# Moving y's second half by one token: shift products on TensorE replaced by transfers from SBUF to SBUF

## The chip, the cores and the metric

The kernel runs on one core of a Trainium2 chip. The metric is the device time of one execution in microseconds (us), taken as the median of several runs; lower is better.

## The reference

Three blocks are added to x (4 batches x 512 tokens x 256 channels, float32), each behind a layer normalization: causal self-attention with 16 heads, a linear cross-attention with 16 heads, and two layers of a local-attention transformer. Only the two layers matter here. Each of them does, for its input x:

```
def shift_token(t):
    t1, t2 = jnp.split(t, 2, axis=-1)
    t2 = jnp.pad(t2, ((0, 0), (1, 0), (0, 0)))[:, :-1]
    return jnp.concatenate([t1, t2], axis=-1)

h = shift_token(x);  q, k, v = split(h @ wqkv);  ...        # 8 heads, windows of 128 tokens
x = x + local_attention(q, k, v) @ wo
h = shift_token(x)                                          # the move that is changed
h = (h - h.mean(-1)) / sqrt(h.var(-1) + 1e-05) * lg + lb
a, g = split(h @ w1 + b1);  x = x + (a * gelu(g)) @ w2 + b2
```

shift_token moves the second 128 channels of every token down by one token: token n gets those of token n - 1, and token 0 gets zeros.

## The kernel before, in words

The two layers run as eight steps m = 0 to 7, one per layer and batch. y, the running x of the layers, lies in SBUF as 128 partitions x 4 batches x 4 token tiles x 256 channels: token 128 t + p is partition p of tile t. A step projects q, k, v, does four pairs of heads (scores in two parts Sa and Sb, exponentials, transposes T in two halves, values AV), sums the pairs into the output product wo in two halves of two token tiles, and adds each half to y (`add_to_y`, L1382 on VectorE). The MLP of the step follows interleaved with the next step's attention: statistics, shift, normalization into hn, transposes of hn (hnT), the first product w1 with its gates, the second product w2.

The move by one token is a matter of partitions, which VectorE and ScalarE do not cross, so before the change TensorE does it. `shifted_half` (L1827, L1829) multiplies y's second halves by a matrix that has ones one place off the diagonal, and a second product carries partition 127 of tile t to partition 0 of tile t + 1. The result is a bank of PSUM called "sh". `mlp_stats` takes the statistics of the first half from y (L1390), `mlp_norm` those of the second half from the bank (L1396) and joins them (L1399); GpSimd makes rstd (`mlp_rstd`, L806 and L808); `mlp_apply` writes hn, the second half from the bank (L1408) and the first from y (L1412).

Every engine works through one list written out by hand, in order: a START, UNIT and ENTRY list for the first two blocks, then STEP_PE, STEP_DVE, STEP_ACT and STEP_POOL, repeated for each step with a lead (@1 is the next step's item, @-1 the last one's), and CLOSE lists for the end. An item whose input is not there stops all that stand behind it on its engine. Banks of PSUM go round in groups: "g" (2, 5, 6, 7) serves q, k, v, wo, w1, w2, AV and sh in the order of TensorE's list, "t" (3, 4) the transposes. In PSUM banks 0 and 1 Sb of a pair follows Sa, and TensorE may write Sb only when VectorE has read Sa.

SyncE issues all transfers, on one queue, in the order of its program: it loads layer 1's weights as the last products of layer 0 are done, reads x2 back, and stores y. It too stops at each wait. hn shares its place in SBUF with hnT and with the gates gl of the MLP; VectorE has read the last of them before it adds the next step's output sums.

Of the kernel before, what the change touches and what calls it, by code (L numbers as in the profile page):

```python
# [10 lines left out]
ALU = mybir.AluOpType  # L11
# [3 lines left out]
P = 128  # L15
# [51 lines left out]
def constants():  # L67

    ident = np.eye(P, dtype=np.float32)
    i = np.arange(P)[:, None]  # L70
    j = np.arange(P)[None, :]
    causal = np.zeros((P, S), np.float32)
    causal[:, S - P:] = np.where(j <= i, 0.0, NEG)
    local = np.concatenate([np.where(i <= j, 0.0, NEG), np.where(j <= i, 0.0, NEG)], 1).astype(np.float32)
    heads = (i // XDH == j // XDH).astype(np.float32)
    half = np.arange(0, FDH, 2, dtype=np.float32)
    inv_freq = (1.0 / np.float32(10000.0) ** (half / np.float32(FDH))).astype(np.float32)
    t = np.arange(S, dtype=np.float32)
    freqs = t[:, None] * inv_freq[None, :]
    freqs = np.concatenate([freqs, freqs], -1)  # L80
    base = ((half + np.float32(0.4 * FDH)) / np.float32(1.4 * FDH)).astype(np.float32)
    power = ((t - S // 2) / np.float32(W // 2)).astype(np.float32)
    scale = (base[None, :] ** power[:, None]).astype(np.float32)
    scale = np.concatenate([scale, scale], -1)
    cos, sin = np.cos(freqs), np.sin(freqs)
    sign = np.where(np.arange(FDH) < FDH // 2, -1.0, 1.0).astype(np.float32)
    rot = np.stack([cos * scale, sin * sign * scale, cos / scale, sin * sign / scale])
    rot = rot.reshape(4, T, P, FDH).transpose(2, 0, 1, 3).astype(np.float32)
    shift = np.zeros((P, 2, P), np.float32)
    shift[:, 0, :] = i == j - 1  # L90
    shift[P - 1, 1, 0] = 1.0
    return {"c_ident": ident, "c_causal": causal, "c_local": local, "c_heads": heads, "c_shift": shift,
            "c_rot": np.ascontiguousarray(rot)}


def build(nc, a, out, x2_dram, w_dram, tab_dram):

    with ExitStack() as ctx:
        def sem(name):
            return ctx.enter_context(nc.semaphore(name))  # L100
# [102 lines left out]
        b1 = sbt(ctx, "b1", [P, DEPTH, 2, NF])  # L203
        shift = sbt(ctx, "shift", [P, 2, P])
        hnT_hi = sbt(ctx, "hnT_hi", [P, E2, S], F32R)
# [103 lines left out]
        def unit_at(u):  # L309
# [29 lines left out]
        ENTRY_DVE = ("sA.30 r.29.0 z.28 sB.30 r.29.1 pk.31 t.29.0 t.29.2 pq.31 t.29.4 sA.31 r.30.0 z.29 sB.31 "  # L339
# [21 lines left out]
        STEP_PE = ("q2@1 hnT@-1 v2@1 k2@1 Ta1 Sa3 hid0@-1 Tb1 hid1@-1 Tqk1@1 Sb3 hid2@-1 q3@1 hid3@-1 k3@1 "  # L361
                   "Tqk2@1 hid4@-1 hid5@-1 AV1 Ta2 v3@1 hT@2 w20@-1 Tqk3@1 q0@2 Tb2 Sa0@1 AV2 Sb0@1 k0@2 "
                   "Ta3 q1@2 w21@-1 Tb3 k1@2 Sa1@1 AV3 Sb1@1 Ta0@1 wo0 wo1 v0@2 sh Tb0@1 v1@2 Sa2@1 AV0@1 "
                   "Sb2@1 Tqk0@2")
        STEP_DVE = ("Tqk3 Tb2@-1 Sa0 fb3@-1 q0@1 w20@-2 Sb0 k0@1 Ta3@-1 q1@1 w21@-2 Tb3@-1 fa0 Sa1 k1@1 Sb1 "
# [3 lines left out]
        STEP_ACT = ("Tqk0@1 AV0 q2@1 v1@1 hnT@-1 ea2 k2@1 Ta1 v2@1 eb2 Tb1 hid0@-1 hs0@-1 hid1@-1 Tqk1@1 "  # L369
                    "hid2@-1 hs1@-1 hs2@-1 q3@1 hid3@-1 k3@1 Tqk2@1 hs3@-1 hid4@-1 hid5@-1 hs4@-1 hs5@-1 Ta2 "  # L370
# [3 lines left out]
        CLOSE_PE = ("T.29.0 hnT.6 Sa.31 T.29.1 w1.6.0 w1.6.1 Sb.31 AV.29 T.30.0 w1.6.2 T.30.1 w1.6.3 w1.6.4 "  # L374
                    "AV.30 T.31.0 wo_early.7.0 T.31.1 w1.6.5 AV.31 wo_early.7.1 wo.7.0 wo.7.1 sh.7 w2.6.0 "
                    "hnT.7 w2.6.1 w1.7.0 w1.7.1 w1.7.2 w1.7.3 w1.7.4 w1.7.5 w2.7.0 w2.7.1")
        CLOSE_DVE = ("soft.27.1 Tqk.7.3 w2.5.0 T.26.1 Sa.28 T.27.0 Sb.28 T.27.1 soft.28.0 Sa.29 Sb.29 w2.5.1 "
# [6 lines left out]
        CLOSE_ACT = ("AV.28 T.29.0 hnT.6 T.29.1 exp.30.0 w1.6.0 w1.6.1 exp.30.1 AV.29 T.30.0 exp.31.0 w1.6.2 "  # L384
                     "w1.6.3 T.30.1 exp.31.1 AV.30 T.31.0 hs.6.0 w1.6.4 hs.6.1 T.31.1 w1.6.5 hs.6.2 hs.6.3 "
                     "AV.31 hs.6.4 hs.6.5 hnT.7 w1.7.0 hs.7.0 w1.7.1 w1.7.2 w1.7.3 hs.7.1 w1.7.4 hs.7.2 "
                     "hs.7.3 w1.7.5 hs.7.4 hs.7.5")
        CLOSE_POOL = ("sum.0 soft.30.1 soft.31.0 soft.31.1 last.6 norm.7 last.7 sum.1")
        MLP = ("stats", "sh", "norm", "apply", "hnT", "hT")

# [83 lines left out]
        for what, *at in pe_order:  # L474
# [31 lines left out]
            if what == "w1":  # L506
# [3 lines left out]
                else:  # L510
                    plan["w1a", at[0], at[1]] = plan["w1g", at[0], at[1]]
            if what == "sh":
                turn(("sh", *at), "g")
            if what == "Tqk":
# [42 lines left out]
        def _(sp):  # L557
# [115 lines left out]
            for l in range(DEPTH):  # L673
                sp.dma_start(lng[:, l, :], a["ln_g"][l]).then_inc(ld_small, 16)
                sp.dma_start(lnb[:, l, :], a["ln_b"][l]).then_inc(ld_small, 16)
                sp.dma_start(b1[:, l, :, :], a["b1"][l]).then_inc(ld_small, 16)
            sp.dma_start(shift[:, :, :], a["c_shift"]).then_inc(ld_shift, 16)

            wait_full(sp, plan["q", B - 1, T - 1])
            layer_wqkv_lo(1, 0)  # L680
# [9 lines left out]
            layer_wqkv_hi(1, 2)  # L690
            for tp in range(2):
                wait_read(sp, plan["wo", B - 1, tp])
            layer_wo(1)
            wait_full(sp, plan["w1a", B - 1, NF - 1])
            layer_w1(1)
            for tp in range(2):
                wait_full(sp, plan["w2", B - 1, tp])
            layer_w2(1)
            wait_full(sp, plan["v", STEPS - 1, T - 1])
            sp.wait_ge(l_ssm, 2 * T * STEPS)  # L700
            for b in range(B):
# [377 lines left out]
        def _(dve):  # L1079
# [312 lines left out]
            def mlp_norm(m):  # L1392

                bank = wait_full(dve, plan["sh", m])
                for t in range(T):
                    dve.bn_stats(stats[:, 0, t, 6:12], bank[:, t * P:(t + 1) * P]).then_inc(f_stats, 1)  # L1396
                dve.wait_ge(f_stats, 2 * T * (m + 1))
                for t in range(T):
                    dve.bn_aggr(mv[:, 0, t, :], stats[:, 0, t, :]).then_inc(f_mv, 1)  # L1399

            def mlp_apply(m):
                b = m % B
                dve.wait_ge(f_mv, T * (m + 1))
                dve.wait_ge(f_rstd, m + 1)
                use = plan["sh", m]
                bank = psum[use[0]]
                for t in range(T):
                    ins = dve.tensor_scalar(hn[:, t, P:D], bank[:, t * P:(t + 1) * P], mv[:, 0, t, 0:1],  # L1408
                                            rstd[:, 0, t:t + 1], ALU.subtract, ALU.mult)
                ins.then_inc(read[use[0]], 1)  # L1410
                for t in range(T):
# [114 lines left out]
        def _(pe):  # L1526
# [291 lines left out]

            def shifted_half(m):

                if m == 0:
                    pe.wait_ge(ld_shift, 16)
                for tp in range(2):
                    wait_read(pe, plan["wo", m, tp])
                use = plan["sh", m]
                bank = wait_free(pe, use)
                mm(bank[:, :].rearrange("p (t e) -> p t e", e=P), shift[:, 0, :], y[:, m % B, :, P:D], start=True,  # L1827
                   stop=False, skip_group_check=True)
                mm(bank[:, P:T * P].rearrange("p (t e) -> p t e", e=P), shift[:, 1, :], y[:, m % B, 0:T - 1, P:D],  # L1829
                   start=False, stop=True, skip_group_check=True).then_inc(full[use[0]], 1)  # L1830

            def transposed_norm(m):
# [38 lines left out]
            for what, *at in pe_order:  # L1871
# [40 lines left out]
                if what == "wo":  # L1912
                    output_part(*at, range(FPAIRS - 1, FPAIRS) if at[0] == STEPS - 1 else range(FPAIRS))
                if what == "sh":
                    shifted_half(*at)
                if what == "hnT":
# [81 lines left out]
```

## Time and profile before

| | us |
|---|---|
| median of three runs | 1153.77 (1152.77 to 1156.58) |
| the profiled execution's own time | 1154.38 |
| its span, first to last instruction | 1152.6 |
| TensorE busy | 1124.3 (98%) |
| VectorE busy | 790.9 (69%) |
| ScalarE busy | 691.6 (60%) |
| GpSimd busy | 610.0 (53%) |

The span is what the profile's times count in; the execution's own time has 1.8 us more around it. The chain that ended last is 90% TensorE. The first two blocks end at about 600 us; the eight steps take the rest, and their output sums are added to y at 612, 688, 764, 840, 916, 992, 1061 and 1107 us.

### The profile page before, as it was taken

The page shows a single profiled execution, that of the slowest core. Times are in us where ns is not written, and L with a number is a line of the kernel's source. Part 1 is how long each engine was busy: PE and PEld are TensorE (multiplying, and loading weights), DVE is VectorE, ACT ScalarE, POOL GpSimd, SP SyncE. Part 2 cuts the span into 40 slices and gives each one's busy share as a digit, 9 for nine tenths or more (in the row PEclk, how much of TensorE's full clock was granted, in tenths as well). Part 3 has the DMA queues.
Part 4 walks back from the last instruction along what each step waited for, and adds up shares of the span by engine and source line. Part 5 has one row for each costly group of instructions (what it writes and reads, how often), then busy time and mean ns, then how long its engine had stood idle before and what let it go on. Part 6 is the DMA issues. An engine that isn't in the chain of part 4 may idle for free.

```text
span 1152.6 us, 20639 instructions
## 1 busy us (share of the span) xinstructions
PE 1124.3 (98%) x7114; PEld 874.4 (76%) x7114; DVE 790.9 (69%) x2417; ACT 691.6 (60%) x1712; POOL 610.0 (53%) x641
## 2 busy tenths in 40 slices
PE   8999999999999999999999999999999999999997
PEld 6777777777777766767667887877878878787676
DVE  6867677667767356778897677768667686675553
ACT  3668677777767224453676647657656566575832
POOL 1456666666664322049896446557465474573330
PEclk9999999999999999999999999999999999999999
DMA  7003333323210401030040001200002100001010
GB/s 255 1 2 132 100 109 113 123 93 123 89 71 2 164 19 55 1 112 22 19 176 1 2 1 36 94 1 1 1 19 99 55 1 1 1 32 42 19 38 18
DMA packets 30310, 64.72 MB, mean 56 GB/s; under 512 B 3840, under 2 KB 16256, under 8 KB 29696
## 3 DMA queue, kind: packets, MB, share of 16 engines
q1 hardware_dynamic: 30208, 63.41, 15.7%
q8 instruction: 58, 0.95, 0.3%
q14 instruction: 44, 0.36, 0.1%
HBM read 41.04 MB, written 22.36 MB: 55 GB/s over the span
## 4 chain that ended last, share of the span: by engine, by line
PE 90%; DVE 4%; POOL 2%; ACT 2%; issue 1%; DMA 0%; DVEq 0%; ACTq 0%; POOLq 0%
PE psum L1532 48%; PE psum L1633 7%; PE psum L1598 6%; PE psum L1615 6%; PE psum L1765 5%; PE psum L1814 5%; PE psum L1799 4%; PE psum L1781 4%; PE psum L1747 2%; PE psum L1827 1%; PE psum L1838 1%; PE psum L1721 1%; POOL rn L780 1%; PE psum L1829 0%; DVE y L1091 0%
## 5 line engine op out<-in xcount | busy, mean ns | idle before, releaser
L735 POOL TENSOR_TENSOR probs<-probs,rden 128x128 f32<-128x128 f32 (+3 forms) x256 | 177.6, 725 | 80.6 <-DVE rden L1149 80.6
L974 ACT ACTIVATE lp<-lp,lneg,rn 128x256 f32<-128x256 f32 (+1 forms) x256 | 143.6, 568 | 11.6 <-DVE lneg L1366 11.5
L890 ACT ACTIVATE probs<-probs,negmax 128x128 f32<-128x128 f32 (+3 forms) x256 | 139.9, 553 | 5.8 <-DVE negmax L1144 5.8
L1134 DVE CUSTOM_DVE_ANT_0 probs<-psum,causal 128x128 f32<-128x128 f32 (+3 forms) x256 | 110.3, 487 | 19.4 <-PE psum L1598 19.3
L768 POOL TENSOR_TENSOR lp<-lp,lrden 128x128 f32<-128x128 f32 x64 | 25.6, 400 | 165.8 <-DVE lrden L1371 165.8
L780 POOL TENSOR_TENSOR rn<-ssm,neg_half 128x8 f32<-128x8 f32 x64 | 108.4, 1693 | 0.0
L1354 DVE CUSTOM_DVE_ANT_0 lp<-psum,local 128x256 f32<-128x256 f32 (+1 forms) x256 | 84.2, 385 | 20.6 <-PE psum L1765 20.6
L771 POOL TENSOR_TENSOR lp<-lp,lrden 128x768 f32<-128x768 f32 x64 | 93.9, 1467 | 0.0
L1532 PE MATMUL psum<-wqkv_hi,hT_lo 128*128 128x512 f32 x192 | 82.0, 427 | 0.1
L961 ACT ACTIVATE sq<-psum 128x512 f32<-128x512 f32 x64 | 38.0, 594 | 68.9 <-PE psum L1532 68.9
L1633 PE MATMUL psum<-pT,v 128*64 128x256 f32 (+3 forms) x512 | 77.7, 446 | 1.4 <-DVE pT L1158 1.0
L1615 PE MATMUL psum<-ident,probs 128*128 128x128 f32 x640 | 75.9, 273 | 2.4 <-POOL probs L735 1.7
L1615 PEld LDWEIGHTS psum<-ident,probs 128*128 128x128 f32 x640 | 71.5, 141 | 7.9 <-POOL probs L735 3.0
L1532 PE MATMUL psum<-wqkv_hi,hT_hi 128*128 128x512 f32 x192 | 75.8, 395 | 0.0
L1532 PE MATMUL psum<-wqkv_lo,hT_hi 128*128 128x512 f32 x192 | 75.3, 392 | 0.0
L858 ACT ACTIVATE lpT<-psum 128x512 f32<-128x512 f32 x64 | 38.1, 595 | 61.1 <-PE psum L1781 60.8
L1532 PE MATMUL psum<-hnT_lo,w_hi 128*124 128x512 f32 (+2 forms) x176 | 71.9, 408 | 0.8 <-DVE hnT_lo L1343 0.8
L1158 DVE COPY pT<-psum 128x512 f32<-128x512 f32 (+1 forms) x96 | 54.6, 596 | 25.6 <-PE psum L1615 25.4
L741 POOL TENSOR_TENSOR w_rest<-w_raw,w_half 128x760 fp32r<-128x760 f32 x22 | 39.9, 1814 | 61.0 <-ACT w_half L858 61.0
L1633 PEld LDWEIGHTS psum<-pT,v 128*64 128x64 f32 x512 | 35.7, 138 | 44.6 <-issue 36.7
L1532 PE MATMUL psum<-hnT_hi,w_hi 128*124 128x512 f32 (+2 forms) x176 | 69.4, 394 | 0.0
L1532 PE MATMUL psum<-hnT_hi,w_lo 128*124 128x512 f32 (+2 forms) x176 | 69.4, 394 | 0.0
(172 smaller groups left out, 3146.7 us busy)
## 6 DMA issues: line engine op xcount, KB each, us to landing
w_raw<-in_w_all SPq DMA_DIRECT2D x22, 380.0 KB, 3.1
w_scratch<-w_half SPq DMA_DIRECT2D x22, 380.0 KB, 2.3
w_scratch<-w_rest SPq DMA_DIRECT2D x22, 380.0 KB, 3.0
x<-in_x SPq DMA_DIRECT2D x8, 512.0 KB, 7.4
aw<-in_w_quads SPq DMA_DIRECT2D x4, 768.0 KB, 5.5
wqkv_lo<-w_scratch SPq DMA_DIRECT2D x6, 512.0 KB, 6.3
wqkv_hi<-w_scratch SPq DMA_DIRECT2D x6, 512.0 KB, 4.5
w_hi<-w_scratch SPq DMA_DIRECT2D x2, 1364.0 KB, 6.5
```

Of the source, the lines that this page charges most:

```text
L735: ins = pool.tensor_tensor(pr, pr, rden[:, u % 2, h, i:i + 1].broadcast_to([P, TRI[i]]), ALU.mult)
L771: pool.tensor_tensor(pr, pr, r, ALU.mult).then_inc(l_prob, 1)
L780: pool.tensor_tensor(rn[:, m % 2, t, i, :], ssm[:, i, :], neg_half[:, 0:FH], ALU.pow).then_inc(l_rn, 1)
L890: ins = act.activation(pr, pr, ACT.Exp, bias=negmax[:, u % 2, h, i:i + 1], scale=ADH ** -0.5, accum_out=den[:, u % 2, h, i:i + 1])
L974: ins = act.activation(pr, pr, ACT.Exp, bias=lneg[:, u % 2, h, w:w + 1], scale=rn[:, m % 2, w, 0, 2 * j + h:2 * j + h + 1], accum_out=lden ...
L1134: ins = dve.tensor_tensor_reduce(probs[:, u % 2, h, TRI_AT[i]:TRI_AT[i + 1]], bank[:, at:at + TRI[i]], causal[:, S - TRI[i]:S], 1.0, -3e38 ...
L1354: ins = dve.tensor_tensor_reduce(lp[:, u % 2, h, lo:hi], bank[:, at:at + hi - lo], local[:, LOC - (hi - lo):LOC], 1.0, -3e38, ALU.add, ALU ...
L1532: ins = mm(dst, lhsT, rhs, start=i == 0, stop=i == len(pairs) - 1, **kw)
L1598: ins = mm(banks_of[h][:, at:at + n], kt[rows, cols], qt[rows, 0:n], start=term == 0, stop=term == 2)
L1615: ins = pe.transpose(bank[:, at:at + P], probs[:, u % 2, h, lo:lo + P], ident[:, :])
L1633: ins = mm(bank[rows, c * P:S], v[:, b % 2, c, cols], pT[:, h, KEYB_AT[c]:KEYB_AT[c] + KEYB[c]], start=c == 0, stop=c == T - 1)
L1765: ins = mm(pair[h][:, at:at + n].rearrange("p (w k) -> p w k", k=P), lqT[rows, c, d, :], keys[rows], start=True, stop=True)
```

## The change

The shift matrix, its load, the two products, their bank and the list item "sh" go. SyncE moves y's second half straight into hn instead, in two halves: when an output sum has been added to y, one transfer carries partitions 0 to 126 of its two token tiles to partitions 1 to 127, and partition 127 of each tile goes to partition 0 of the next tile in a transfer of its own; a row of zeros from memory fills token 0. Six transfers per step count one semaphore up by 16 each, and `mlp_norm` waits for all of them. Statistics and normalization of the second half then read and write hn in place.

```diff
+            def move_half(m):
+                b = m % B
+                for tp in range(2):
+                    wait_read(sp, plan["wo", m, tp])
+                    ts = slice(2 * tp, 2 * tp + 2)
+                    sp.dma_start(hn[1:P, ts, P:D], y[0:P - 1, b, ts, P:D]).then_inc(y_moved, 16)
+                    for t in range(2 * tp, min(2 * tp + 2, T - 1)):
+                        sp.dma_start(hn[0:1, t + 1, P:D], y[P - 1:P, b, t, P:D]).then_inc(y_moved, 16)
+                    if tp == 0:
+                        sp.dma_start(hn[0:1, 0, P:D], a["c_zero"]).then_inc(y_moved, 16)
+            move_half(0)
+            move_half(1)
             wait_full(sp, plan["q", B - 1, T - 1])
             layer_wqkv_lo(1, 0)
...
             layer_wqkv_hi(1, 2)
-            for tp in range(2):
-                wait_read(sp, plan["wo", B - 1, tp])
+            move_half(2)
+            move_half(3)
             layer_wo(1)
...
             layer_w2(1)
+            move_half(4)
+            move_half(5)
             wait_full(sp, plan["v", STEPS - 1, T - 1])
...
+            move_half(6)
+            move_half(7)
             for b in range(B):
                 dst = out[b].rearrange("(t p) e -> p t e", p=P)
...
             def mlp_norm(m):
-                bank = wait_full(dve, plan["sh", m])
+                dve.wait_ge(y_moved, 6 * 16 * (m + 1))
                 for t in range(T):
-                    dve.bn_stats(stats[:, 0, t, 6:12], bank[:, t * P:(t + 1) * P]).then_inc(f_stats, 1)
+                    dve.bn_stats(stats[:, 0, t, 6:12], hn[:, t, P:D]).then_inc(f_stats, 1)
...
-                    ins = dve.tensor_scalar(hn[:, t, P:D], bank[:, t * P:(t + 1) * P], mv[:, 0, t, 0:1],
-                                            rstd[:, 0, t:t + 1], ALU.subtract, ALU.mult)
-                ins.then_inc(read[use[0]], 1)
+                    dve.tensor_scalar(hn[:, t, P:D], hn[:, t, P:D], mv[:, 0, t, 0:1], rstd[:, 0, t:t + 1],
+                                      ALU.subtract, ALU.mult)
...
-            def shifted_half(m):
-                if m == 0:
-                    pe.wait_ge(ld_shift, 16)
-                for tp in range(2):
-                    wait_read(pe, plan["wo", m, tp])
-                use = plan["sh", m]
-                bank = wait_free(pe, use)
-                mm(bank[:, :].rearrange("p (t e) -> p t e", e=P), shift[:, 0, :], y[:, m % B, :, P:D], start=True,
-                   stop=False, skip_group_check=True)
-                mm(bank[:, P:T * P].rearrange("p (t e) -> p t e", e=P), shift[:, 1, :], y[:, m % B, 0:T - 1, P:D],
-                   start=False, stop=True, skip_group_check=True).then_inc(full[use[0]], 1)
```

The lists change with it, in few places (the stretches around the change, before and after):

```diff
-STEP_PE  ... q3@1 hid3@-1 k3@1 Tqk2@1 hid4@-1 ... Ta0@1 wo0 wo1 v0@2 sh Tb0@1 v1@2 Sa2@1 AV0@1 Sb2@1 Tqk0@2
+STEP_PE  ... q3@1 hid3@-1 Tqk2@1 k3@1 hid4@-1 ... Ta0@1 wo0 wo1 v0@2 Tb0@1 v1@2 Sa2@1 Tqk0@2 AV0@1 Sb2@1
-STEP_DVE ... wo0@-1 fb0 wo1@-1 fa1 stats@-1 Ta0 norm@-1 Tb0 Sa2 apply@-1 Tqk0@1 fb1 Sb2 ... hs5@-1 fb2 Ta2
+STEP_DVE ... wo0@-1 fb0 wo1@-1 fa1 stats@-1 Ta0 Tb0 norm@-1 Sa2 apply@-1 Tqk0@1 fb1 Sb2 ... hid3@-1 fb2 k3@1
-STEP_ACT Tqk0@1 AV0 q2@1 v1@1 hnT@-1 ea2 ...
+STEP_ACT Tqk0@1 v1@1 hnT@-1 AV0 q2@1 ea2 ...
-CLOSE_PE ... wo.7.0 wo.7.1 sh.7 w2.6.0 hnT.7 w2.6.1 ...
+CLOSE_PE ... wo.7.0 wo.7.1 w2.6.0 hnT.7 w2.6.1 ...
```

In CLOSE_DVE the output sums and statistics of step 6 move by a few places among the pairs' items, in CLOSE_ACT T.30.0 goes ahead of AV.29.

## Rows read from the trace of the kernel before

**Rows 1.** Busy us by stage: PE, PEld, DVE, ACT, POOL; granted clock, DMA share, GB/s.

```profile
680.00:748.00 68.00, 68.00 (x418) 54.78 (x417) 48.98 (x149) 41.81 (x98) 39.32 (x34) 1.00 0.16 55
```

**Rows 2.** The chain of waits, 688 to 699 us: start us, us, what, count.

```profile
688.54 0.86 PE psum L1827 x2
689.40 0.65 PE psum L1829 x2
690.05 0.76 PE psum L1781 x7
690.81 1.39 PE psum L1532 x6
692.20 0.86 PE psum L1765 x8
693.05 1.67 PE psum L1799 x16
694.72 1.06 PE psum L1765 x8
695.78 1.02 PE psum L1747 x8
...
698.19 0.87 PE psum L1838 x8
```

**Rows 3.** VectorE in order of time, end of step 1: start, us, instruction, idle before.

```profile
683.75 0.69 DVE L1382 TENSOR_TENSOR y<-psum,y 128x512 f32<-128x512 f32 x1 [2.04 <-PE psum L1814]
...
687.20 0.69 DVE L1382 TENSOR_TENSOR y<-psum,y 128x512 f32<-128x512 f32 x1 [2.68 <-PE psum L1814]
...
690.09 0.89 DVE L1396 BATCH_NORM_STATS2 stats<-psum 128x6 f32<-128x128 f32 x4 [0.76 <-PE psum L1829]
691.01 0.42 DVE L1399 BATCH_NORM_AGGREGATE mv<-stats 128x2 f32<-128x12 f32 x4
...
693.09 0.29 DVE L1354 CUSTOM_DVE_ANT_0 lp<-psum,local 128x128 f32<-128x128 f32 x1 [1.23 <-PE psum L1765]
...
694.20 1.36 DVE L1408 TENSOR_SCALAR hn<-psum,mv,rstd 128x128 f32<-128x128 f32 x4
695.49 1.10 DVE L1412 TENSOR_SCALAR hn<-y,mv,rstd 128x128 f32<-128x128 f32 x4
```

**Rows 4.** GpSimd in order of time, the same microseconds.

```profile
691.84 1.04 POOL L808 TENSOR_TENSOR rstd<-rstd,neg_half 128x4 f32<-128x4 f32 x1
```

**Rows 5.** DMA: the last store of y alone, 1149.9 to 1152.7 us; the queue's total.

```profile
DMA packets 272, 0.26 MB, mean 94 GB/s; under 512 B 16, under 2 KB 272, under 8 KB 272
out<-y SPq DMA_DIRECT2D x1, 256.0 KB, 2.1
...
q1 hardware_dynamic: 30208, 63.41, 15.7%
```

**Rows 6.** DMA queue: packets, MB, engines' share; 334.9:335.7 (256 B), 1081.5:1082.7 (1 KB).

```profile
q1 hardware_dynamic: 449, 0.11, 59.5%
...
q1 hardware_dynamic: 402, 0.41, 100.3%
```

**Rows 7.** Busy us by stage, the last step's second MLP products (columns as rows 1).

```profile
1138.80:1142.00 3.20, 3.13 (x14) 3.14 (x15) 0.01 (x1) 0.00 (x0) 0.00 (x0) 0.50 0.00 0
...
1108.40:1113.00 4.60, 4.60 (x38) 4.44 (x36) 2.51 (x13) 0.00 (x0) 1.26 (x2) 1.00 0.00 0
```

**Rows 8.** VectorE and TensorE in order of time, step 7.

```profile
1105.52 0.69 DVE L1382 TENSOR_TENSOR y<-psum,y 128x512 f32<-128x512 f32 x1 [1.14 <-PE psum L1814]
...
1108.95 0.89 DVE L1396 BATCH_NORM_STATS2 stats<-psum 128x6 f32<-128x128 f32 x4 [0.51 <-PE psum L1829]
...
1120.24 0.49 PE L1532 MATMUL psum<-hnT_lo,w_hi 128*124 128x512 f32 x1 [0.54 <-DVE hnT_lo L1343]
...
1138.87 0.58 PE L1532 MATMUL psum<-w_hi,hid_lo 124*128 124x256 f32 x1 [3.01 <-DVE hid_lo L1437]
```

**Rows 9.** The page's 40 slices: busy share of the DMA engines in tenths.

```profile
DMA  7003333323210401030040001200002100001010
```

More of the change, by code:

```diff
@@ L88, in constants @@
     rot = rot.reshape(4, T, P, FDH).transpose(2, 0, 1, 3).astype(np.float32)
[L89 to L92, printed above, removed]
+    return {"c_ident": ident, "c_causal": causal, "c_local": local, "c_heads": heads, "c_zero": np.zeros((1, P), np.float32),
             "c_rot": np.ascontiguousarray(rot)}
@@ L203, in build @@
         b1 = sbt(ctx, "b1", [P, DEPTH, 2, NF])
-        shift = sbt(ctx, "shift", [P, 2, P])
         hnT_hi = sbt(ctx, "hnT_hi", [P, E2, S], F32R)
@@ L277, in build @@
         set1 = sem("set1")
-        ld_shift = sem("ld_shift")
+        y_moved = sem("y_moved")
         hid_one, last_gate = sem("hid_one"), sem("last_gate")
@@ L360, in build @@
                       "norm.0 k.2.1 soft.5.1 q.2.2 k.2.2 q.2.3 soft.6.0")
[L361 to L364, printed above, removed]
+        STEP_PE = ("q2@1 hnT@-1 v2@1 k2@1 Ta1 Sa3 hid0@-1 Tb1 hid1@-1 Tqk1@1 Sb3 hid2@-1 q3@1 hid3@-1 "
+                   "Tqk2@1 k3@1 hid4@-1 hid5@-1 AV1 Ta2 v3@1 hT@2 w20@-1 Tqk3@1 q0@2 Tb2 Sa0@1 AV2 Sb0@1 "
+                   "k0@2 Ta3 q1@2 w21@-1 Tb3 k1@2 Sa1@1 AV3 Sb1@1 Ta0@1 wo0 wo1 v0@2 Tb0@1 v1@2 Sa2@1 "
+                   "Tqk0@2 AV0@1 Sb2@1")
         STEP_DVE = ("Tqk3 Tb2@-1 Sa0 fb3@-1 q0@1 w20@-2 Sb0 k0@1 Ta3@-1 q1@1 w21@-2 Tb3@-1 fa0 Sa1 k1@1 Sb1 "
[1 row of a table removed]
[1 row of a table added]
                     "Ta1 k2@1 Tb1 Sa3 Tqk1@1 hid0@-1 Sb3 hs0@-1 hid1@-1 hid2@-1 hs1@-1 q3@1 hs2@-1 fa2 "
[1 row of a table removed]
-        STEP_ACT = ("Tqk0@1 AV0 q2@1 v1@1 hnT@-1 ea2 k2@1 Ta1 v2@1 eb2 Tb1 hid0@-1 hs0@-1 hid1@-1 Tqk1@1 "
[1 row of a table added]
+        STEP_ACT = ("Tqk0@1 v1@1 hnT@-1 AV0 q2@1 ea2 k2@1 Ta1 v2@1 eb2 Tb1 hid0@-1 hs0@-1 hid1@-1 Tqk1@1 "
                     "hid2@-1 hs1@-1 hs2@-1 q3@1 hid3@-1 k3@1 Tqk2@1 hs3@-1 hid4@-1 hid5@-1 hs4@-1 hs5@-1 Ta2 "
@@ L374, in build @@
         CLOSE_PE = ("T.29.0 hnT.6 Sa.31 T.29.1 w1.6.0 w1.6.1 Sb.31 AV.29 T.30.0 w1.6.2 T.30.1 w1.6.3 w1.6.4 "
-                    "AV.30 T.31.0 wo_early.7.0 T.31.1 w1.6.5 AV.31 wo_early.7.1 wo.7.0 wo.7.1 sh.7 w2.6.0 "
-                    "hnT.7 w2.6.1 w1.7.0 w1.7.1 w1.7.2 w1.7.3 w1.7.4 w1.7.5 w2.7.0 w2.7.1")
+                    "AV.30 T.31.0 wo_early.7.0 T.31.1 w1.6.5 AV.31 wo_early.7.1 wo.7.0 wo.7.1 w2.6.0 hnT.7 "
+                    "w2.6.1 w1.7.0 w1.7.1 w1.7.2 w1.7.3 w1.7.4 w1.7.5 w2.7.0 w2.7.1")
         CLOSE_DVE = ("soft.27.1 Tqk.7.3 w2.5.0 T.26.1 Sa.28 T.27.0 Sb.28 T.27.1 soft.28.0 Sa.29 Sb.29 w2.5.1 "
[1 row of a table removed]
[1 row of a table added]
                      "soft.29.1 Sb.30 hnT.6 soft.30.0 Sa.31 w1.6.0 T.29.1 w1.6.1 Sb.31 soft.30.1 T.30.0 "
@@ L383, in build @@
                      "w2.7.0 w2.7.1")
-        CLOSE_ACT = ("AV.28 T.29.0 hnT.6 T.29.1 exp.30.0 w1.6.0 w1.6.1 exp.30.1 AV.29 T.30.0 exp.31.0 w1.6.2 "
+        CLOSE_ACT = ("AV.28 T.29.0 hnT.6 T.29.1 exp.30.0 w1.6.0 w1.6.1 exp.30.1 T.30.0 AV.29 exp.31.0 w1.6.2 "
                      "w1.6.3 T.30.1 exp.31.1 AV.30 T.31.0 hs.6.0 w1.6.4 hs.6.1 T.31.1 w1.6.5 hs.6.2 hs.6.3 "
@@ L388, in build @@
         CLOSE_POOL = ("sum.0 soft.30.1 soft.31.0 soft.31.1 last.6 norm.7 last.7 sum.1")
-        MLP = ("stats", "sh", "norm", "apply", "hnT", "hT")
+        MLP = ("stats", "norm", "apply", "hnT", "hT")
         def step_items(cycle, m):
@@ L511, in build @@
                     plan["w1a", at[0], at[1]] = plan["w1g", at[0], at[1]]
-            if what == "sh":
-                turn(("sh", *at), "g")
             if what == "Tqk":
@@ L676, in _ @@
                 sp.dma_start(b1[:, l, :, :], a["b1"][l]).then_inc(ld_small, 16)
-            sp.dma_start(shift[:, :, :], a["c_shift"]).then_inc(ld_shift, 16)
+            def move_half(m):
[10 more added lines that the diff above has]
+            move_half(1)
             wait_full(sp, plan["q", B - 1, T - 1])
@@ L1404, in mlp_apply @@
                 dve.wait_ge(f_rstd, m + 1)
-                use = plan["sh", m]
-                bank = psum[use[0]]
                 for t in range(T):
-                    ins = dve.tensor_scalar(hn[:, t, P:D], bank[:, t * P:(t + 1) * P], mv[:, 0, t, 0:1],
-                                            rstd[:, 0, t:t + 1], ALU.subtract, ALU.mult)
-                ins.then_inc(read[use[0]], 1)
+                    dve.tensor_scalar(hn[:, t, P:D], hn[:, t, P:D], mv[:, 0, t, 0:1], rstd[:, 0, t:t + 1],
+                                      ALU.subtract, ALU.mult)
                 for t in range(T):
@@ L1817, in output_part @@
                     ins.then_inc(full[use[0]], 1)
-            def shifted_half(m):
-                if m == 0:
-                    pe.wait_ge(ld_shift, 16)
-                for tp in range(2):
-                    wait_read(pe, plan["wo", m, tp])
-                use = plan["sh", m]
-                bank = wait_free(pe, use)
-                mm(bank[:, :].rearrange("p (t e) -> p t e", e=P), shift[:, 0, :], y[:, m % B, :, P:D], start=True,
-                   stop=False, skip_group_check=True)
-                mm(bank[:, P:T * P].rearrange("p (t e) -> p t e", e=P), shift[:, 1, :], y[:, m % B, 0:T - 1, P:D],
-                   start=False, stop=True, skip_group_check=True).then_inc(full[use[0]], 1)
             def transposed_norm(m):
@@ L1913, in _ @@
                     output_part(*at, range(FPAIRS - 1, FPAIRS) if at[0] == STEPS - 1 else range(FPAIRS))
-                if what == "sh":
-                    shifted_half(*at)
                 if what == "hnT":
```

9 rows, old and new, of tables (CLOSE_DVE, ENTRY_PE, STEP_DVE) are left out of this document.

## The prediction

> **What bounds the kernel now.** I read the busy times by stage first. In the stretch that holds one whole step of the local-attention layers, TensorE is busy for all of its 68.0 us, and VectorE for 49.0 [rows 1]; here the reader sees that a step lasts as long as TensorE's list of work, and that anything which makes TensorE wait is paid in full, since it has no slack in which to catch up. Next the chain of waits for 688 to 698 us, the end of step m = 1 and the start of the next: it holds nothing but TensorE, and in it the two shift products, 0.86 + 0.65 = 1.51 us [rows 2]. Then VectorE's and GpSimd's rows of the same microseconds [rows 3, 4]: the first output sum is added to y from 683.75 to 684.44, the second from 687.20 to 687.89, the statistics of the shifted half begin at 690.09, the aggregates at 691.01, rstd is there at 692.88, and hn is written from 694.20. What counts is that VectorE works in a written order: behind the shifted half's statistics stand Sa (the masked scores of the next pair), the writing of hn, and every copy of the next step.
>
> **What the change removes.** Sixteen shift products (two each for eight steps), 1.51 us of TensorE per step. In seven steps TensorE is the bound, so this is worth up to 7 x 1.51 = 10.6 us. In step 7 TensorE waits for hn's way anyway (0.54 us before w1 [rows 8]), so there it is worth nothing by itself. Writing hn's second half from SBUF instead of PSUM: four instructions took 1.36 us from PSUM [rows 3]; the bounds are 0 and the 0.26 by which the four from y beside them are shorter, and I take 0.2.
>
> **What it adds.** Six transfers per step on SP's queue, and a wait for all six in front of the shifted half's statistics. Four are single rows of 512 B. The other two carry 127 rows x 2 token tiles, 254 pieces of 512 B each, one when each output sum has been added. The trace has no transfer from SBUF to SBUF and none of 127 rows, so I bound it.
>
> Lower end: it goes like the 256 KB store of y, which is 128 rows x 2 tiles, 256 pieces of 1 KB. That landed 2.1 us after its issue with 272 packets, which is 256 pieces and 16 closing ones [rows 5]: sixteen engines with 16 pieces and one closing packet each. Upper end: one engine does all 254. What the rows say on the choice: in the whole program the queue moved 30208 packets, exactly 16 x 1888 [rows 5], so transfers of 128 rows (16 x 8) are cut in equal shares. 127 is prime: whole rows in equal shares go only into one share (or 127). Whether the hardware would cut 127 unevenly (fifteen eights and a seven) no row shows. I take the one share, since only equal shares are seen and none other is to be had.
>
> The Trainium skill, page "DMA: Bandwidth & Descriptors", section "Why a DMA increments its semaphore by 16 and not by 1", says that such a transfer uses the largest number of engines up to 16 which divides the slowest dimension of both sides, and names 127 partitions as a case of one engine. By that rule the sum is the one below, against the sixteen-engine sum of rival A; the trace agrees as far as its 128-row transfers go, and no run here shows 127.
>
> Price of a piece of 512 B on one engine, from the nearest sizes [rows 6]: 256 B pieces: 449 in 0.8 us on 16 engines at 59.5% busy, 17.0 ns of busy time each and one per engine every 28.5 ns; 1 KB pieces: 402 in 1.2 us at full share, 47.8 ns each. A third of the way between them is 27.3 ns by busy time and 34.9 ns by spacing. I take 30 ns, with 17 and 47.8 as ends. Both transfers of a step use the same engine, so the second waits for the first: 508 pieces and a handful of closing packets, 512 x 30 ns = 15.4 us. What lies around it: the store's 2.1 us less its 17 packets at 47.8 ns (0.8) leaves 1.3 us.
>
> **The sum for a middle step (times of m = 1).** First issue 684.44 + 1.3 + 15.4 = 701.1 us landing; the statistics start then instead of at 690.09, 11.0 us later. TensorE, without the shift, runs from 688.54: T 0.76, v 1.39, Sa 0.86, q/k transposes 1.02 (now ahead of the values), values 1.67 [rows 2], and stands at 694.24 before Sb, whose banks VectorE has not read: statistics 0.92, aggregates about 0.35, Sa 1.11 [rows 3], so 701.1 + 2.4 = 703.5. That is an idle stretch of 9.3 us. Then its clock: after the 3.0 us idle before the last product [rows 8] the granted clock was 0.50, the lower level of 1.2 GHz, for 3.2 us with 14 matmuls, where the same kind of product at full clock did 38 in 4.6 us [rows 7]: 3.2 - 14 x 0.121 = 1.5 us lost per long idle. Sb 1.06 and q (six products like v's, 1.39) then take 3.95, until 707.45. hn is not later than that: rstd comes 2.79 after the statistics' start [rows 3, 4], writing hn 2.4 (694.20 to 696.59) less 0.2, and the copy behind it 0.7 (128x512 out of PSUM, like y's sum), so about 701.1 + 5.7 = 706.8. The transposes of hn start at 707.45 instead of 698.19: 9.3 us later, the removed 1.51 already counted in. What follows hangs on them and shifts with them. Steps 0 to 6: 7 x 9.3 = 65 us.
>
> Step 7 [rows 8]: first sum added at 1106.21, landing at 1106.21 + 16.7 = 1122.9, the statistics 14.0 us later than 1108.95; TensorE has only the first half of the second MLP product in between. hn is 13.8 later; the slow clock adds 1.5 to the next product, of which the 0.54 us wait before w1 hides a part. In all 14.8 us.
>
> Sum: 65 + 14.8 = 80 us on the profiled execution's own 1154.4 us: 1234 us. That execution lies 0.6 us above the median of the three runs, less than any term here.
>
> **Parts costed at nothing.** Transposes of q and k ahead of the values, and T's copy ahead of the statistics on VectorE: the bank of those transposes is free only after that copy, which the new order puts first; if it did not, TensorE would stand one product earlier for the same landing. O's copy behind hn's on ScalarE: the copy takes 0.6 us and its bank is asked for again after q, v and k. "g" banks: 31 takes per step instead of 32, in a stretch where TensorE has no idle time to lose [rows 1]. GpSimd waits with rstd in its list, but the item behind it waits for VectorE's item behind the statistics anyway. On SP the layer-1 weight loads and the final stores stand behind moves: the loads are wanted by the next layer's step tens of microseconds later, and the first store of y waits for step 7's move, with nothing behind it but other stores. Transfers of weights ahead of a move in the queue: most slices after the twentieth show the DMA engines at 0 to 2 tenths [rows 9], so I take 0, and up to 5 us for one step if one collides.
>
> **Rivals.**
> A, the other side: sixteen shares after all. Then each half lands 2.1 us after issue [rows 5], the second at 687.89 + 2.1 = 690.0, where the statistics start today. hn is ready at 690.0 + 5.7 = 695.7, and TensorE asks at 688.54 + 5.70 + 2.45 = 696.7: no wait, 1.51 us gained in seven steps; step 7 gets its second half at 1109.2, 0.2 later than now, against 0.2 of shorter writing. 1154.4 - 10.6 = 1144 us. It decides from 1.0 us of lateness on: a landing after 691.0 starts to eat the gain, one after 692.5 has eaten it. For it: half of the bytes of the store; against it: 127 does not divide.
> B: one engine, but pieces that run faster from SBUF to SBUF, at the 17 to 24 ns end. Each ns is 8 x 0.512 = 4.1 us, so 17 ns gives 1181 and 24 ns 1209. For it: the 17.0 ns of busy time at 256 B; against it: the 28.5 ns spacing in the same row. The Trainium skill, same page, section "Why small descriptors are slow (HBM only)", says that SBUF-to-SBUF transfers don't pay the penalty of small pieces, and its specification table gives some 27 GiB/s an engine; an estimate from that page is 18 ns, 1185 us. No run here shows it.
> C: one engine at the 1 KB price, above 42 ns: 1283 to 1307 us. For it: a piece may be priced by its round trip; against it: half the bytes.
> D: sixteen shares, and a landing that eats the gain: 1150 to 1158 us.
>
> **Chances.** Forecast (24 to 42 ns, 1209 to 1283): 0.58. B 0.13, C 0.09, A 0.16, D 0.04. Slower 0.80, faster 0.16, same 0.04; 0.3%, some 3.5 us, is about what a measurement of this kernel can tell. The range runs from B's end into C, 1183 to 1300 us, and leaves out A, D and a part of C.
>
> **What would show it.** The shifted half's statistics wait for a DMA some 11 us in seven steps and 14 in the last; the moves' first half lands about 9 us after issue, the second about 13; TensorE idles some 9 us before Sb in each step with a granted clock of 0.5 behind it; the DMA share in these 16 us is about one sixteenth. A landing of 2 to 3 us and no such wait make the forecast wrong and A right.

## The result, and the profile after

The changed kernel takes 1236.11 us in the median of four runs (1234.84 to 1236.33), the kernel before 1153.27 us beside it: a ratio of 1.0722 [1.0703, 1.0742], slower by 83 us. The forecast was 1234 us in a range of 1183 to 1300.

The page of the kernel after, in part: the span, TensorE's busy time, three rows of the 40 slices, the queue's packets, and what share of the chain that ended last goes by which engine.

```profile
span 1234.5 us, 20612 instructions
PE 1135.3 (92%) x7082; PEld 882.5 (71%) x7082; DVE 792.4 (64%) x2417; ACT 689.3 (56%) x1712; POOL 617.1 (50%) x641
...
PE   8999999999999999998979799799799798895947
...
PEclk9999999999999999999989989899899899897978
DMA  6003333233204010210400012000021000020010
...
q1 hardware_dynamic: 34928, 65.38, 15.3%
...
PE 78%; DVE 6%; DMA 5%; SPq 5%; POOL 2%; ACT 2%; issue 2%; DVEq 0%; ACTq 0%; POOLq 0%
```

From the second half of the span on, where the eight steps lie, TensorE has gaps and its clock falls in places; before, a middle step had no gap at all. The stretch in [rows 1] is 68 us long and so not the whole step that the prediction calls it, which lasts 75.93 us; over 76 us of the kernel before it is the same (columns as [rows 1]):

```profile
764.00:840.00 76.00, 76.00 (x481) 60.90 (x480) 54.22 (x165) 46.80 (x112) 44.20 (x39) 1.00 0.00 1
```

TensorE is busy 11 us longer than before although its shift products, 8 x 1.51 us, are gone: part of its work now runs at the lower clock. The DMA row stays as empty as before [rows 9]: the transfers are few bytes. The chain now holds DMA and SPq (SyncE's issuing), which it did not need before.

The waits of the whole program, VectorE's first and then TensorE's (who waited, for whom, us in total, times, the longest):

```profile
DVE stats L1406 <- DMA hn<-y: 79.0, 8, 13.1
```

```profile
PE psum L1772 <- DVE lmax L1364: 58.4, 9, 11.8
PE psum L1832 <- DVE hn L1419: 14.3, 1, 14.3
```

The two belong together. VectorE waits for the moves in front of the shifted half's statistics (L1406), 79.0 us in eight steps. Sa stands behind them in its list, and TensorE may not write Sb (L1772) before it: 58 us in all, and 14.3 us more in step 7, where hn's transposes (L1832) wait themselves.

The chain of waits at the end of step m = 1, which answers to [rows 2] (start us, us, what):

```profile
692.79 0.70 DVE y L1392
693.50 0.02 issue
693.51 0.72 SPq L677
694.23 0.04 issue
694.28 4.56 SPq L679
...
699.99 0.74 SPq L677
700.73 0.04 issue
700.78 7.85 DMA hn<-y
708.63 0.02 issue
708.65 0.88 DVE stats L1406 x4
...
711.19 2.08 PE psum L1772 x8
713.26 2.86 PE psum L1539 x6
716.12 1.43 PE psum L1832 x8
```

Where [rows 2] held nothing but TensorE, this chain leaves it for 18 us. The first sum is in y at 693.49. SyncE issues the 127 rows (L677), and then stands 4.56 us in issuing a crossing row (L679); the second 127 rows go out only at 699.99, though their sum was in at 696.94. The last of them lands at 708.63, 15.1 us after the first issue. The last three rows are at the lower clock: 2.08, 2.86 and 1.43 us for what took 1.06, 1.39 (v, of the same form) and 0.87 in [rows 2].

TensorE and VectorE in order of time at the same place; the bracket is the idle time before and what ended it. The second answers to [rows 3].

```profile
698.43 0.55 PE L1788 MATMUL psum<-ident,lp 128*128 128x128 f32 x3 [0.39 <-DVE lpT L1386]
...
711.19 2.08 PE L1772 MATMUL psum<-lkT,lqT 64*128 64x256 f32 x8 [7.29 <-DVE lmax L1364]
```

```profile
708.65 0.87 DVE L1406 BATCH_NORM_STATS2 stats<-hn 128x6 f32<-128x128 f32 x4 [9.08 <-DMA hn<-y]
```

Two stretches of windows (columns as [rows 1]): one whole step, and what follows the idle time.

```profile
697.00:783.00 86.00, 78.27 (x478) 62.41 (x477) 55.46 (x168) 46.50 (x112) 45.46 (x40) 0.94 0.14 47
...
711.00:717.00 6.00, 5.81 (x20) 4.39 (x21) 4.87 (x22) 0.00 (x0) 2.99 (x4) 0.50 0.00 0
```

And the queue while the moves run, 703.2 to 707.2 us (GB/s in 40 slices of 0.1 us; packets, MB, share of 16 engines):

```profile
GB/s 20 20 20 26 20 20 20 26 20 20 20 26 20 20 20 26 20 20 20 26 20 20 20 26 20 20 20 26 20 20 20 26 26 20 20 26 20 20 20 26
...
q1 hardware_dynamic: 200, 0.09, 7.5%
```

An even 22 GB/s at 7.5% of sixteen engines, where one engine is 6.25%: the packets' time adds up to 1.2 engines, as if one worked and the other fifteen hardly at all. The section on 113 + 14 rows counts the engines. 512 B at 22 GB/s are 23 ns a piece, 5.9 us for one half of 254. The whole move, 693 to 709 us (GB/s in 40 slices of 0.4 us):

```profile
GB/s 0 0 0 0 4 12 14 10 14 22 22 22 22 22 22 22 22 24 22 22 22 62 18 10 10 22 22 22 22 22 22 22 22 23 22 22 22 17 0 0
```

From the first data at 694.9 to the last at 708.1 it is 13.2 us for 508 pieces, 26.0 ns each: the queue starts slowly and dips at about 702 us, at the change from one half to the other (the 62 holds one packet of 16 KB on the queue named "instruction").

The steps counted from one "first half's statistics" to the next: 75.93 us before in each of the middle steps, 85.3 to 85.6 after. From step 0 on the differences are +10.5, +9.6, +9.5, +9.7, +9.4, +9.9, +10.2 and, for step 7 up to the end, +14.7 us; the stretch ahead of the first move is 1.5 us shorter, which is no more than it differs between kernels that are alike there (609.9 to 612.7 us). In all 82.0 us.

### The profile page after: what moved, and what is told of

It is laid out like the page before. It is cut to its first block, busy times and chain, and to the rows that moved or that the text cites. A ratio compares the mean times of both kernels' runs of the same rounds, so it can differ in the third digit from the quotient of the medians.

```text
span 1234.5 us, 20612 instructions
## 1 busy us (share of the span) xinstructions
PE 1135.3 (92%) x7082; PEld 882.5 (71%) x7082; DVE 792.4 (64%) x2417; ACT 689.3 (56%) x1712; POOL 617.1 (50%) x641
## 3 DMA queue, kind: packets, MB, share of 16 engines
q1 hardware_dynamic: 34928, 65.38, 15.3%
## 4 chain that ended last, share of the span: by engine, by line
PE 78%; DVE 6%; DMA 5%; SPq 5%; POOL 2%; ACT 2%; issue 2%; DVEq 0%; ACTq 0%; POOLq 0%
PE psum L1539 43%; PE psum L1640 6%; PE psum L1605 6%; PE psum L1622 5%; DMA hn<-y 5%; PE psum L1772 5%; SPq L679 3%; PE psum L1788 3%; PE psum L1806 3%; PE psum L1821 2%; PE psum L1754 1%; PE psum L1546 1%; SPq L677 1%; PE psum L1832 1%; DVE lp L1364 1%
## 5 line engine op out<-in xcount | busy, mean ns | idle before, releaser
L1772 PE MATMUL psum<-lkT,lqT 64*128 64x256 f32 (+1 forms) x512 | 72.5, 405 | 58.4 <-DVE lmax L1364 58.4
L790 POOL TENSOR_TENSOR rn<-ssm,neg_half 128x8 f32<-128x8 f32 x64 | 113.3, 1771 | 0.0
L778 POOL TENSOR_TENSOR lp<-lp,lrden 128x128 f32<-128x128 f32 x64 | 28.3, 442 | 157.6 <-DVE lrden L1381 157.6
L781 POOL TENSOR_TENSOR lp<-lp,lrden 128x768 f32<-128x768 f32 x64 | 96.6, 1509 | 0.0
L1772 PEld LDWEIGHTS psum<-lkT,lqT 64*128 64x128 f32 x512 | 43.0, 201 | 74.9 <-DVE lmax L1364 59.9
L1539 PE MATMUL psum<-wqkv_hi,hT_lo 128*128 128x512 f32 x192 | 85.9, 447 | 0.1
L1539 PE MATMUL psum<-wqkv_hi,hT_hi 128*128 128x512 f32 x192 | 78.5, 409 | 0.0
L1539 PE MATMUL psum<-wqkv_lo,hT_hi 128*128 128x512 f32 x192 | 78.1, 407 | 0.0
L1010 ACT ACTIVATE hnT<-psum,lnb,lng 128x512 f32<-128x512 f32 x16 | 12.4, 778 | 116.0 <-PE psum L1832 116.0
```

What stands on the lines that cost most here:

```text
L781: pool.tensor_tensor(pr, pr, r, ALU.mult).then_inc(l_prob, 1)
L790: pool.tensor_tensor(rn[:, m % 2, t, i, :], ssm[:, i, :], neg_half[:, 0:FH], ALU.pow).then_inc(l_rn, 1)
L1539: ins = mm(dst, lhsT, rhs, start=i == 0, stop=i == len(pairs) - 1, **kw)
L1772: ins = mm(pair[h][:, at:at + n].rearrange("p (w k) -> p w k", k=P), lqT[rows, c, d, :], keys[rows], start=True, stop=True)
```

## The experiments

My theory: 127 rows are cut over one engine, and everything else follows from this late landing. Two rivals stayed possible: that the transfers are slow as such (six issues, SyncE's queue, SBUF to SBUF), however they are cut; and that the changed lists are to blame. Each run below stands beside runs of the kernel before on the same chip.

### 127 rows as 112 + 15, and as 122 + 5

The same bytes, with more transfers. 112 = 16 x 7 and 15 go into 16 and 15 equal shares, 122 = 2 x 61 only into two.

```diff
-sp.dma_start(hn[1:P, ts, P:D], y[0:P - 1, b, ts, P:D]).then_inc(y_moved, 16)
+for lo, hi in ((0, 112), (112, P - 1)):        # second kernel: (0, 122), (122, P - 1)
+    sp.dma_start(hn[lo + 1:hi + 1, ts, P:D], y[lo:hi, b, ts, P:D]).then_inc(y_moved, 16)
...
-dve.wait_ge(y_moved, 6 * 16 * (m + 1))
+dve.wait_ge(y_moved, 8 * 16 * (m + 1))
```

> The 127 rows of each half go as 112 and 15 rows, everything else as in the changed kernel; two transfers more per half. Theory (the cost is that 127 rows make one share on one engine): 112 is 16 x 7, so the 224 pieces go over sixteen engines; the last landing of a half comes about 2.3 us after its output sum, VectorE waits under 1 us for it, TensorE does not idle before Sb, the granted clock stays at 1.0: 1143 to 1148 us. Rival 1 (a transfer from SBUF to SBUF in 512 B pieces moves at some 23 GB/s however it is shared): landing 15 us after the first issue as now, 1236 us. Rival 2 (SyncE's issuing is the cost, six transfers take it 12 us per step): eight transfers take longer, above 1236 us.

Measured: 1159.21 us, ratio 1.0048 [1.0032, 1.0063]: 77 us less than with 127 rows, as the theory says, but 11 us above the expected range. What is missing lies at the edges (the move left out, below). VectorE's wait for the moves, and the queue in 0.6 us of them:

```profile
DVE stats L1407 <- DMA hn<-y: 14.2, 8, 6.0
```

```profile
q1 hardware_dynamic: 196, 0.10, 64.6%
```

> The 127 rows go as 122 and 5. Theory of equal shares: the largest number up to 16 that divides 122 is 2, so two engines with 122 pieces each per half; at the 23 ns per piece of the changed kernel that is 2.8 us of moving, landing 4 to 5 us after the second output sum, VectorE's wait some 2 us, 1153 to 1162 us. If the split of rows were uneven over sixteen engines in general and 127 slow for another reason: 1144 us. Rivals 1 and 2: 1236 us and more.

Measured: 1173.07 us, ratio 1.0160 [1.0147, 1.0174], also 11 us above the range; VectorE's wait is 3.8 us per step where 2 were expected. The same wait there:

```profile
DVE stats L1407 <- DMA hn<-y: 30.6, 8, 8.2
```

The wait goes from 79.0 to 30.6 and 14.2 us with one, two and sixteen engines (64.6% of all sixteen, where one alone would be 6.25%), and the time with it. Of the 89.6 us that the transfers cost in all (the run without them, below) 76.9 go by cutting 127 alone. The rival of slow transfers as such is left with the rest, 12.7 us.

### 113 + 14

The control: also two transfers per half, but 113 is prime as 127 is.

```diff
-    for lo, hi in ((0, 112), (112, P - 1)):
+    for lo, hi in ((0, 113), (113, P - 1)):
```

> As the kernel with 112 and 15 rows, with one row shifted between the two transfers: 113 and 14. Same bytes, same number of transfers. Theory of equal shares: 113 is prime, so its 226 pieces per half go over one engine at 23 ns, the last landing 13 to 15 us after the first issue, VectorE waits 7 to 9 us per step: 1220 to 1240 us. Rivals (number of transfers, bytes, SyncE's issuing, or any price per piece that does not ask how rows divide): 1159 us, as 112 and 15.

Measured: 1232.2 us, ratio 1.0685 [1.0667, 1.0703]. The wait, and the queue from 703 to 706 us:

```profile
DVE stats L1407 <- DMA hn<-y: 75.1, 8, 12.7
```

```profile
q1 hardware_dynamic: 197, 0.08, 9.7%
```

One row shifted from the first transfer to the second is worth 73 us: 1159 with 112, 1232 with 113. So it is neither the size nor the number of the transfers, but how the number of rows divides. SyncE, by the way, stands here in issuing the second transfer of a half, the 14 rows (the line holds the 113 and the 14):

```profile
693.29 4.58 SPq L678 DMA_DIRECT2D hn<-y  x2
```

The packets count the engines without any timing. The 256 KB store had its 256 pieces and 16 closing packets more, which the prediction reads as one for each engine [rows 5]. The queue's packets with 112 + 15, 122 + 5 and 113 + 14 rows, in this order:

```profile
q1 hardware_dynamic: 35408, 65.38, 16.4%
...
q1 hardware_dynamic: 35024, 65.38, 16.2%
...
q1 hardware_dynamic: 35152, 65.38, 15.4%
```

The pieces are the same in all of them and in the kernel after (34928). Over the sixteen halves of the program the three have 30, 6 and 14 packets per half more than it. These are the closing packets of 16 + 15, 2 + 5 and 1 + 14 engines, less one. So the reading holds, and 127 rows have one closing packet and one engine. Were they split unevenly over sixteen engines, they would have sixteen, and 112 + 15 could not add 30.

### The move left out

The second half stays unshifted: statistics and normalization read it from y. This is what the kernel would take if the move were free.

```diff
-sp.dma_start(hn[1:P, ts, P:D], y[0:P - 1, b, ts, P:D]).then_inc(y_moved, 16)
...
-dve.bn_stats(stats[:, 0, t, 6:12], hn[:, t, P:D]).then_inc(f_stats, 1)
+dve.bn_stats(stats[:, 0, t, 6:12], y[:, m % B, t, P:D]).then_inc(f_stats, 1)
```

> Leaves the move out: the normalization reads y's second half where it lies, so the tokens of the second half are not shifted; no transfers and no wait, the lists as in the changed kernel. It prices the removed products alone: seven times 1.51 us and 0.7 us in the last step, 1141 to 1144 us. If it comes out near 1153, the products were never on the path and the loss is all there is; if above 1160, the lists themselves cost.

Measured: 1146.5 us, ratio 0.9931 [0.9918, 0.9944], 2.5 us above the expected range. The removed products are worth 8 us in all, not the 10.6 that 7 x 1.51 give. A middle step takes 75.42 us, 0.5 less than before, where 1.51 us of TensorE left. And the kernel with 112 + 15 has the same 75.42: in steps 1 to 5 its move is hidden wholly. What it is longer by lies at the edges: +2.2 us in step 0, +3.3 in step 6, +10.0 in step 7 to the end (the profiled execution of 112 + 15, 1162.32 us, is the longest of its six, 3 us above their median, so that these edges may be the long ones).

### The lists alone

The kernel before with the changed lists; the shift products stay, their item "sh" at its old place.

```diff
-STEP_PE  ... q3@1 hid3@-1 k3@1 Tqk2@1 hid4@-1 ... sh Tb0@1 v1@2 Sa2@1 AV0@1 Sb2@1 Tqk0@2
+STEP_PE  ... q3@1 hid3@-1 Tqk2@1 k3@1 hid4@-1 ... sh Tb0@1 v1@2 Sa2@1 Tqk0@2 AV0@1 Sb2@1
-STEP_DVE ... stats@-1 Ta0 norm@-1 Tb0 Sa2 ...
+STEP_DVE ... stats@-1 Ta0 Tb0 norm@-1 Sa2 ...
```

> The kernel before with the changed lists, the shift products put back at their place (behind v0, ahead of T's second half). Theory: the moved items cost nothing, 1151 to 1156 us. Rival 3 (the q/k transposes ahead of the values and the statistics behind T's second copy cost by themselves): above 1160 us.

Measured: 1157.42 us, ratio 1.0024 [1.0015, 1.0033], 1.4 us above the expected range and far from the 83 us of the change. The lists cost 2.9 us, and a middle step 76.51 instead of 75.93 us. TensorE's wait for the lower part of hn's transposes, which the kernel before has in two steps (0.8 us), stands in seven:

```profile
PE psum L1531 <- DVE hnT_lo L1342: 1.8, 7, 0.6
```

In a middle step this wait is 0.2 of the 0.6 us. The run without the move lacks 1.0 us per step of the 1.51 that were removed. 0.4 of it is a wait that its trace shows and the kernel after has too (698.43, above): T's second half waits for a bank until VectorE has copied T's first half out of it. In the kernel before, the shift products stood between the two halves of T and covered that copy. Of the rest the lists are a part: beside the moves they cost 0.2 us per step and not 0.6 (75.4 against 75.2 us, in the last experiment). What the other 0.4 us or so are, no run here shows.

### Fewer transfers: the whole move behind the second sum

If the edges are SyncE's issuing, fewer issues must help there. One transfer of 112 rows x 4 tiles, one of 15 rows x 4, one of the three crossing rows, all behind the second sum; the zero row behind the first.

```diff
+wait_read(sp, plan["wo", m, 0])
+sp.dma_start(hn[0:1, 0, P:D], a["c_zero"]).then_inc(y_moved, 16)
+wait_read(sp, plan["wo", m, 1])
+for lo, hi in ((0, 112), (112, P - 1)):
+    sp.dma_start(hn[lo + 1:hi + 1, :, P:D], y[lo:hi, b, :, P:D]).then_inc(y_moved, 16)
+sp.dma_start(hn[0:1, 1:T, P:D], y[P - 1:P, b, 0:T - 1, P:D]).then_inc(y_moved, 16)
```

> Four transfers per step instead of eight: the row of zeros is issued behind the first output sum, and behind the second 112 rows x 4 tiles, 15 rows x 4 tiles and one transfer for the three crossing rows. Theory 2 (what 112 and 15 rows still lose against the kernel before is SyncE's issuing of eight transfers, 7 us in the last step where both sums come within 1 us): the last landing comes some 3.5 us after the second sum in every step; the last step gains 3 to 4 us, steps 0 and 6 about 1 us each: 1153 to 1156 us. Rival (the loss is the time to land, whatever is issued): 1159 us.

Measured: 1157.66 us, ratio 1.0032 [1.0020, 1.0045], above the expected range; the intervals of this kernel and of 112 + 15 by halves overlap, so the total does not decide between theory and rival. In the profiled executions step 7 is 3.8 us shorter, as expected (48.8 instead of 52.6 us), but steps 0 and 6 are not shorter: 0.2 and 1.1 us longer. VectorE's wait in step 7 is half as long as with eight transfers (first line: eight, second: four):

```profile
1114.76 0.87 DVE L1407 BATCH_NORM_STATS2 stats<-hn 128x6 f32<-128x128 f32 x4 [6.01 <-DMA hn<-y]
...
1111.12 0.87 DVE L1404 BATCH_NORM_STATS2 stats<-hn 128x6 f32<-128x128 f32 x4 [3.25 <-DMA hn<-y]
```

But it still is there: in step 7 the sums come 0.86 us apart, TensorE has half a product to do beside the move, and the issues alone take 1.60 + 0.73 us. TensorE then waits 4.5 us for hn (7.2 with eight transfers, 1.1 before), and the granted clock is 0.50 from 1114.6 to 1121.2 us.

### Moves in steps 1 to 5, products in steps 0, 6 and 7

What the runs point to: moves as in the last experiment where a step hides them, shift products at the edges. First with the lists of before, but T's second copy ahead of the shifted half's statistics on VectorE; then with the changed step lists.

```diff
+MOVED = range(1, 6)
...
-"wo0@-1 fb0 wo1@-1 fa1 stats@-1 Ta0 norm@-1 Tb0 Sa2 apply@-1 Tqk0@1 fb1 Sb2 hnT@-1 q2@1 "
+"wo0@-1 fb0 wo1@-1 fa1 stats@-1 Ta0 Tb0 norm@-1 Sa2 apply@-1 Tqk0@1 fb1 Sb2 hnT@-1 q2@1 "
...
+if m in MOVED:
+    dve.wait_ge(y_moved, 4 * 16 * (m - MOVED[0] + 1))
+else:
+    bank = wait_full(dve, plan["sh", m])
```

> The kernel before with the move by transfers (four, as in the whole-move kernel) in steps 1 to 5 alone; steps 0, 6 and 7 keep the shift products. Its lists are those of before but for T's second copy, which goes ahead of the statistics on VectorE. Theory: each of the five steps gains 0.5 to 1.1 us as without any move, nothing is lost in the last steps: 1148 to 1152 us. Rival (without the changed lists the landing shows on TensorE): 1154 us or more.

> As the one before it, with the changed step lists on all engines. If the changed lists cost 0.6 us per step as they did alone, 1151 to 1155 us and 2 to 3 us behind the old lists; if they pay only together with the transfers, not slower than the old lists.

Measured: 1149.75 us, ratio 0.9971 [0.9960, 0.9982], and 1150.86 us, ratio 0.9979 [0.9968, 0.9990]. Both are 0.2 to 0.3% faster than the kernel before, little but clear of the intervals; the two intervals overlap, so which lists are better with it stays open. With the old lists a middle step takes 75.2 us, 0.7 less than before, five times. VectorE's wait for the moves is down to this (with either lists):

```profile
DVE stats L1415 <- DMA hn<-y: 4.3, 5, 1.0
```

## Why the prediction was right, step by step

**One engine for 127 rows: right, and now shown.** 16 equal shares (rival A) would have been 1144 us by the prediction's sum. 112 against 113 rows and the closing packets decide it. The Trainium skill, page "DMA: Bandwidth & Descriptors", section "Why a DMA increments its semaphore by 16 and not by 1", by whose rule only the largest divisor up to 16 counts, agrees with all four cuts: 127 (1236 us), 113 (1232), 122 (1173) and 112 with 15 (1159). Rivals A and D fall with it. One reason that the prediction gave was none: a sum of packets that 16 divides [rows 5] does not tell equal shares over sixteen engines from others, for the kernel after has 34928 = 16 x 2183 with its large moves on one engine. What held was the other reason, that of the numbers up to 16 only 1 divides 127.

**The piece: 30 ns forecast, 26.0 measured over the move, 23 in its even part.** The even part lies in rival B's range; slow start and handover bring the mean into the forecast's own. By that the transfers took 13.2 instead of 15.4 us; the rest around them was 1.9 instead of 1.3. Landing after the first issue: 15.1 against 16.7 us. Rival C, above 42 ns, falls. The estimate of 18 ns in rival B, worked out from the Trainium skill, page "DMA: Bandwidth & Descriptors", section "Specifications", is reached in no run here; the measurement decides.

**Landing to Sb: 2.4 us forecast, 2.54 measured** (708.65 to 711.19).

**The clock: 1.5 us forecast, 3.0 measured.** I took it from one stretch of step 7 whose work ended 3.2 us after it began [rows 7], so that nothing later could be seen there. Here the granted clock stays at 0.50 from 711 to 717 us, six microseconds. Sb and q take 4.94 us instead of 2.45 at full clock, hn's transposes 1.43 instead of 0.87: 2.49 + 0.56 = 3.05. Of this term the size was wrong, by a factor of two.

**The idle time before Sb: 9.3 us forecast, 7.29 measured**, and 0.39 for T's copy before it. Most of the difference is the earlier landing.

**The sum per step: 9.3 forecast, 9.4 to 10.5 measured.** From the first sum's end to hn's transposes it was 13.75 us before (684.44 to 698.19); it is 22.6 now (693.49 to 716.12), and the transposes last 0.56 longer: 9.4. So 1.6 us less of landing and 1.5 us more of slow clock cancelled. That the sum came so near is luck: by the prediction's own 4.1 us per ns, 26.0 ns a piece would have made some 1218 us of its 1234, and the clock, sized at half, made up for most of it. The path was right, and two of its terms were off in opposite ways.

**Step 7: 14.8 us forecast, 14.7 measured.** VectorE's first sum and its wait for the moves, and TensorE's wait for hn:

```profile
1172.80 0.69 DVE L1392 TENSOR_TENSOR y<-psum,y 128x512 f32<-128x512 f32 x1 [1.14 <-PE psum L1821]
...
1188.79 0.87 DVE L1406 BATCH_NORM_STATS2 stats<-hn 128x6 f32<-128x128 f32 x4 [13.06 <-DMA hn<-y]
...
1193.86 1.97 PE L1832 MATMUL psum<-ident,hn 128*128 128x128 f32 x8 [14.29 <-DVE hn L1419]
```

Here too two terms cancelled. Counted from the end of the first sum, the statistics start 12.6 us later than before (14.0 forecast), and what follows hn's transposes loses about 2.4 us where 1.5 less a part was forecast; TensorE works at a granted clock of 0.50 from 1193.9 to 1198.3 us.

**Edits costed at nothing: wrong by about 1 us per step, but behind the cover.** Where TensorE has no other wait, the removed products give 0.5 us per step and not 1.51. 0.4 us of the difference is T's second half waiting for the copy of T's first half. The prediction weighed the order of T's second copy and the statistics; it did not ask what the shift products had covered. The lists cost 0.6 us per step alone and 0.2 beside the moves, and the rest is open. In the kernel after all this lies ahead of a longer wait and costs nothing more. So the gain of rival A was sized too high as well: with a free move it is 8 us, not 10.6.

**SyncE's queue: not seen at all.** The prediction let the second half go out when its sum was added. It went out 3 us later, behind a crossing row in whose issue SyncE stood. As the engine was still at the first half's pieces until about 702 us, this probably cost little here; what it costs alone was not tried.

## What to carry to other kernels

Before a row count of a transfer between partitions is written down, look at its divisors: 127 rows on one engine took 15 us where 112 + 15 were hidden in the middle steps, so cut a prime count into a multiple of sixteen and a rest. An instruction that waits for a transfer holds everything written behind it in its engine's list; here it was Sa, and so TensorE, that paid. A removed product is worth its duration only if nothing it covered comes to light: of 1.51 us per step 0.5 were left, and where the move shows (2.2 us in step 0, 3.3 in step 6, 10.0 in step 7) the product was the cheaper way.

## What the runs showed of the hardware that I had not expected

**An issue can stand for microseconds.** All crossing rows of the kernel after, and of the one with 112 + 15 (duration ns: min/median/max):

```profile
L679 SPq DMA_DIRECT2D hn<-y x24: 590/4546/4692, 608.3 to 1180.9; - x24
```

```profile
L680 SPq DMA_DIRECT2D hn<-y x24: 577/588/1653, 610.5 to 1113.0; - x24
```

The first crossing row behind 127 rows, one row of 512 B, took some 4.5 us to issue (sixteen of the 24) while one engine had 254 pieces to move, and the row right behind it 0.59; with the pieces spread the median is 0.59. All else on the queue stood behind it. The engine had not yet done its pieces by then: the issue ended at 698.83, the first half's pieces at about 702. What the issue waited for, no run shows.

**Issuing has a price of its own.** Where it did not stand, SyncE took 0.58 to 0.99 us for nearly every transfer from SBUF to SBUF, against 0.43 for the zero row out of memory and 0.37 for a store of y in the kernel before. Eight of them in step 7, one behind the other, are 7 us (1106.54 to 1113.59 with 112 + 15), although their pieces are spread.

**The lower clock outlasts the idle time.** After 7.29 us of waiting TensorE ran at a granted clock of 0.50 (1.2 GHz) for six microseconds of dense work, 711 to 717 us; the wait's price is its own length and about 3 us more.
